# Three float32r products in place of one float32 product, in most projections of a four-layer attention kernel, under a new order of the work

## The reference

```
L0: x += proj(causal_attention(q,k,v of ln(x)));  x += proj(cross_attention(q of ln(x), k,v of context))
    x += gelu(ln(x) @ W_fc + b) @ W_mproj + b                       # 256 -> 1024 -> 256
L1: the same shape with layer norms behind the sums, relu, and a general mask in its self-attention
L2: cross-attention (q of x, k,v of context, a mask per element), 16 heads of 16, then layer norm
L3: cross-attention with 16 heads of 64: q = x @ w_q (256 -> 1024), k, v = context @ w_k, w_v (256 -> 1024),
    softmax(q k / 8) v, @ w_fc (1024 -> 256), plus x, then layer norm
```

## Time and profile before

| | us |
|---|---|
| median of 3 runs (4389.6 to 4390.9) | 4390.59 |
| span of the profiled execution | 4385.8 |
| PE busy | 4260.8 (97%) |
| DVE busy | 3663.2 (84%) |
| ACT busy | 2547.7 (58%) |
| POOL busy | 1590.0 (36%) |

### The profile page before, as it was taken

How to read it: one execution, slowest core, us unless ns; L and a number is a source line. 1 busy time by engine, 2 the same in 40 slices (tenths; PEclk the granted TensorE clock), 3 DMA queues, 4 the chain that set the end, 5 groups by cost and what they waited for, 6 DMA issues and landing times. The chain is left out here.

```text
span 4385.8 us, 99261 instructions
## 1 busy us (share of the span) xinstructions
PE 4260.8 (97%) x33536; PEld 3436.5 (78%) x33536; DVE 3663.2 (84%) x12709; ACT 2547.7 (58%) x6753; POOL 1590.0 (36%) x2709
## 2 busy tenths in 40 slices
PE   5999999999999899999999999999999999999998
PEld 3788888888887677777777777778888888888886
DVE  4899999999997899999999999967777777777774
ACT  2556656566565545455454554536676767676765
POOL 3445454454452234444444444431222222222222
PEclk8999999999999999999999999999999999999999
DMA  5555455554553544545444454433222222222220
GB/s 172 147 154 161 133 151 153 140 161 138 149 157 114 152 132 137 141 127 163 133 146 132 133 149 124 135 98 84 62 78 61 79 61 79 61 77 63 72 66 9
DMA packets 406443, 513.40 MB, mean 117 GB/s; under 512 B 133808, under 2 KB 373936, under 8 KB 384432
## 3 DMA queue, kind: packets, MB, share of 16 engines
q1 hardware_dynamic: 398544, 496.82, 39.7%
q10 hardware_dynamic: 7392, 10.24, 0.7%
HBM read 266.30 MB, written 236.72 MB: 115 GB/s over the span
## 5 line engine op out<-in xcount | busy, mean ns | idle before, releaser
L816 ACT ACTIVATE probs_own<-bank 128x384 f32<-128x384 f32 (+2 forms) x1280 | 644.6, 569 | 80.0 <-DVE bank L1065 41.7
L723 ACT ACTIVATE ht<-bank,columns_l 128x256 f32<-128x256 f32 x384 | 197.2, 569 | 729.4 <-PE bank L1242 726.3
L625 POOL TENSOR_SCALAR veps<-meanvar 128x2 f32<-128x2 f32 x256 | 63.9, 249 | 1357.1 <-DVE meanvar L966 1357.1
L1189 PE MATMUL bank<-ht,w_ff 128*128 128x256 f32 x2048 | 489.8, 382 | 2.7 <-ACT ht L723 1.6
L1189 PE MATMUL bank<-w_ff,ffh 128*128 128x256 f32 x2048 | 475.7, 380 | 0.0
L1046 DVE DVE_READ_ACCUMULATOR2_ANT nmf_own<- 128x1 f32 x3072 | 433.5, 141 | 0.0
L1189 PEld LDWEIGHTS bank<-w_ff,ffh 128*128 128x128 f32 x2048 | 378.7, 190 | 49.4 <-issue 1.2
L1046 DVE CUSTOM_DVE_ANT_0 bank<-bank,mask_rows 128x256 f32<-128x256 f32 x1024 | 398.8, 457 | 21.2 <-PE bank L1189 21.1
L1189 PEld LDWEIGHTS bank<-ht,w_ff 128*128 128x128 f32 x2048 | 369.6, 190 | 50.0 <-ACT ht L723 2.8
L1189 PE MATMUL bank<-kstack_own,qstack_own 96*128 96x256 bf16 (+2 forms) x3072 | 370.1, 248 | 27.2 <-DMA kstack_own<-k_parts 18.7
L881 ACT ACTIVATE probs_other<-bank,negmax 128x120 f32<-128x120 f32 x1024 | 356.6, 383 | 59.6 <-DVE negmax L1169 59.6
(11 more groups left out here) (164 smaller groups left out, 10138.4 us busy)
## 6 DMA issues: line engine op xcount, KB each, us to landing
qstack_own<-q_parts SPq DMA_DIRECT2D x96, 768.0 KB, 5.7
kstack_own<-k_parts SPq DMA_DIRECT2D x64, 768.0 KB, 7.3
qstack_other<-q_parts SPq DMA_DIRECT2D x64, 768.0 KB, 5.9
q_parts<-q_parts_own SPq DMA_DIRECT2D x96, 384.0 KB, 2.5
q_parts<-q_parts_own SPq DMA_DIRECT2D x96, 256.0 KB, 2.3
k_parts<-k_parts_own SPq DMA_DIRECT2D x64, 384.0 KB, 2.9
q_parts<-other_parts SPq DMA_DIRECT2D x64, 384.0 KB, 2.5
other_words<-k_parts SPq DMA_DIRECT2D x64, 360.0 KB, 3.3
```

The source lines that it names most:

```text
L625: nc.gpsimd.tensor_scalar(veps[key][:, :], meanvar[key][:, :, 1], r["norms"][key]["eps"], None, ALU.add).then_inc(veps_ready.sem, 1)
L723: return nc.scalar.activation(out, in_, ACT.Identity, scale=scale, bias=bias)
L816: nc.scalar.activation(probs[key][0:rows, j % a.slots, 0:n], bank_of(u)[0:rows, 0:n], ACT.Exp, scale=a.scale).then_inc(a_done.sem, 1)
L1189: return nc.tensor.matmul(out, lhsT, rhs, start=first, stop=True, skip_group_check=True)
```

## The change

Each float32 product `lhsT.T @ rhs` of the listed steps becomes three float32r products into the same PSUM bank: both operands are written as a high part of type float32r and a remainder, lo = x - hi, also float32r, and hi*hi + hi*lo + lo*hi is summed.

```diff
+        def mm3(out, lhsT, rhs, first):
+            mm(out, lhsT[0], rhs[0], first)
+            mm(out, lhsT[0], rhs[1], False)
+            return mm(out, lhsT[1], rhs[0], False)
```

```diff
-                        ins = mm(bank[:, m * T:(m + 1) * T], r["ff"]["w"][:, c, (2 * j + m) * P:(2 * j + m + 1) * P], x[:, c, :], c == 0)
+                        ins = mm3(bank[:, m * T:(m + 1) * T], (hi[:, c, at], lo[:, c, at]), (ht_hi["2"][:, c, :], ht_lo["2"][:, c, :]), c == 0)
```

The parts are made by new steps. Per element: ACT writes `ht_hi` from PSUM ahead of `ht`, and POOL subtracts:

```diff
+                    if key in r["split_ht"]:                      # "0" and "2" in l0 and l1, "1" in l2
+                        affine(ht_hi[key][:, 0, :], bank[:, 0:T], gain[:, 0:1], shift[:, 0:1])
+                        affine(ht_hi[key][:, 1, :], bank[:, T:2 * T], gain[:, 1:2], shift[:, 1:2])
                     affine(ht[key][:, 0, :], bank[:, 0:T], gain[:, 0:1], shift[:, 0:1])
...
+            elif kind == "ht_lo":                                 # POOL
+                for f in range(FT):
+                    ins = nc.gpsimd.tensor_tensor(ht_lo[key][:, f, :], ht[key][:, f, :], ht_hi[key][:, f, :].bitcast(F32), ALU.subtract)
...
+            elif kind == "rest3":                                 # DVE, 4 per element of l2
+                v.tensor_tensor(ot3_lo[:, 2 * j:2 * j + 2, :], bank, ot3_hi[:, 2 * j:2 * j + 2, :].bitcast(F32), ALU.subtract)
```

```diff
+            elif kind == "weights_hi":
+                act_e.wait_ge(arrived[key], ...)
+                for h, x in zip(hi, raw):
+                    ins = copy(h[:, :, :], x[:, :, :])
...
+            elif kind == "weights_lo":
+                        ins = nc.gpsimd.tensor_tensor(lo[n][:, c, :], raw[n][:, c, :], hi[n][:, c, :].bitcast(F32), ALU.subtract)
```

All of `LISTS` is new, for every engine and pass, and `SPREAD` is now (0, 1) throughout, so that the first and last elements of a pass are no longer corrected. A few places, old and new (time in element periods):

```diff
-START = {"l0": 0.0, "l1": 33.12879, "l2": 66.18842}
+START = {"l0": 0.00000, "l1": 32.95726, "l2": 66.42901}
 l0 PE
-            norm.0.0/0.24343 project_k.own.0/0.29714 ... negate_t.own.0/1.16618 ... norm.2.0/3.92324 ff_in.ff.0/3.97118 ... ff_out.ff.3/4.88122
+            norm.0.0/0.60700 project_k.own.0/0.82717 ... negate_t.own.0/1.71999 ... norm.2.0/4.37194 ff_in.ff.1/4.51158 ... ff_out.ff.3/5.45066
 l0 DVE
-            ff_in.ff.3/4.73013 ff_mid.ff.2/4.74993 ff_mid.ff.3/4.80456
+            ff_in.ff.2/5.17545 ff_mid.ff.2/5.27393 ff_in.ff.3/5.32873 ff_mid.ff.3/5.35967
 l1 PE
-            turn.0.0/0.09548 project_q.own.0/0.13496 ... negate_t.own.0/1.17403 ... norm.2.0/3.87252 ff_in.ff.1/3.92875 ... ff_out.ff.3/4.79026
+            turn.0.0/0.14969 project_k.own.0/0.28915 ... negate_t.own.0/1.70805 ... norm.2.0/4.20845 ff_in.ff.3/4.32439 ... ff_out.ff.3/4.92385
 l2 PE
-            ... probs_v3.three.3/3.66090 project_out3.three.2/3.72515 project_out3.three.3/3.76506
+            ... probs_v3.three.2/3.80393 project_out3.three.0/3.96077 ... project_out3.three.3/4.17756
 l2 DVE
-            project_out3.three.0/3.81120 stats.3.0/3.82783 norm.3.0/3.88660
+            rest3.three.1/3.56262 rest3.three.0/3.60038 rest3.three.3/3.89264 rest3.three.2/3.90734 project_out3.three.0/4.21786 stats.3.0/4.51278 norm.3.0/4.86170
```

More of the change, by code:

```diff
@@ L60 @@
         "PE": """
[L61 to L75, removed]
@@ L76 @@
-            probs_v.other.2/3.40602 probs_v.other.3/3.41650 project_out.other.0/3.64697 norm.2.0/3.92324 ff_in.ff.0/3.97118
-            ff_in.ff.1/4.08214 ff_in.ff.2/4.50058 ff_in.ff.3/4.56880 ff_out.ff.0/4.68899 ff_out.ff.1/4.77584 ff_out.ff.2/4.82853
-            ff_out.ff.3/4.88122
+            norm.0.0/0.60700 project_k.own.0/0.82717 project_q.own.0/0.86112 scores_max.own.4/1.28161 scores_max.own.11/1.29911
+            scores_max.own.9/1.30514 scores_max.own.7/1.31117 scores_max.own.2/1.38316 scores_max.own.5/1.43286
@@ L86 @@
[L86 to L90, removed]
@@ L92 @@
+            ff_mid.ff.2/5.19113 ff_in.ff.3/5.20549 ff_mid.ff.3/5.34441
         """,
         "DVE": """
[L94 to L106, removed]
@@ L144 @@
-            scores_exp.other.1/3.08000 scores_exp.other.5/3.08802 probs_v.other.0/3.32424 probs_v.other.1/3.33391
-            probs_v.other.2/3.34357 probs_v.other.3/3.35324 project_out.other.0/3.61110 norm.2.0/3.87252 ff_in.ff.1/3.92875
-            ff_in.ff.2/4.28344 ff_in.ff.0/4.39942 ff_in.ff.3/4.49575 ff_out.ff.0/4.65459 ff_out.ff.1/4.69327 ff_out.ff.2/4.75159
-            ff_out.ff.3/4.79026
+            turn.0.0/0.14969 project_k.own.0/0.28915 project_q.own.0/0.36215 project_v.own.0/1.17639 scores_max.own.0/1.23948
@@ L148 @@
+            probs_v.other.1/3.72375 project_out.other.0/4.00600 norm.2.0/4.20845 ff_in.ff.3/4.32439 ff_in.ff.0/4.40560
+            ff_in.ff.2/4.52839 ff_in.ff.1/4.58809 ff_out.ff.0/4.73628 ff_out.ff.2/4.80963 ff_out.ff.1/4.87757 ff_out.ff.3/4.92385
         """,
         "ACT": """
-            turn.0.0/0.11124 split_hi_q.own.0/0.17966 split_mid_q.own.0/0.23820 split_hi_k.own.0/0.27302
-            split_mid_k.own.0/0.38316 split_hi_k.other.0/1.13125 scores_exp.own.2/1.29684 scores_exp.own.1/1.30749
@@ L177 @@
-            negate.other.1/2.74174 negate.other.2/2.81011 negate.other.3/2.84852 negate_t.other.0/2.90492
-            project_v.other.0/3.21119 probs_v.other.0/3.36405 probs_v.other.1/3.37834 heads_rec.other.0/3.40659
-            heads_back.other.0/3.55262 project_out.other.0/3.67569 stats.2.0/3.70189 norm.2.0/3.79538 ff_out.ff.0/4.83497
-            stats.3.0/4.85109 norm.3.0/4.90957
+            split_rest_k.own.0/0.42105 split_rest_q.own.0/0.43791 project_v.own.0/1.24420 scores_max.own.0/1.26094
@@ L749, in _ @@
                     act_e.wait_ge(a_full.sem, w.value(a_full, u.tag))
+                if first and kind == "norm":
+                    reuse(act_e, w, u, xhat_ready, [("norm", "2", 0)], u.element - 1)
                 for count, tag in ahead["ht_users"][key](a_full, d_full):
@@ L885, in _ @@
                 if first and j == r["first_of"]["turn3"]:
-                    reuse(act_e, w, u, d_full, [("project_out", "other", 0)], u.element - 1)
+                    reuse(act_e, w, u, d_full, [("ff_out", "ff", i) for i in range(4)], u.element - 1)
                 if w.new(a_full, u.tag):
@@ L1427, in _ @@
                     for c in range(2 * j, 2 * j + 2):
-                        ins = mm(bank[:, t * C:(t + 1) * C], x[:, c, t * P:(t + 1) * P], wt[:, c, :], c == 0 and t == 0)
+                        ins = mm(bank[:, t * C:(t + 1) * C], ffh[:, c, t * P:(t + 1) * P], wt[:, c, :], c == 0 and t == 0)
+                ins.then_inc(d_full.sem, 1)
+            elif kind == "project_out3":
+                split("fc")
+                _, (hi,), (lo,) = r["split_weights"]["fc"]
+                if w.new(rest_ready, ("rest3", "three", j)):
+                    pe.wait_ge(rest_ready.sem, w.value(rest_ready, ("rest3", "three", j)))
+                bank = take(u) if j == 0 else bank_of(u, (kind, key, 0))
+                for t in range(QT):
+                    at = slice(t * P, (t + 1) * P)
+                    for c in range(2 * j, 2 * j + 2):
+                        ins = mm3(bank[:, t * C:(t + 1) * C], (ot3_hi[:, c, at], ot3_lo[:, c, at]), (hi[:, c, :], lo[:, c, :]), c == 0 and t == 0)
                 ins.then_inc(d_full.sem, 1)
@@ L1482, in sb, with shared @@
         return t[n]
+    def shared(*tensors):
+        for group in tensors[:-1]:
+            with ExitStack() as one:
+                for n, shape, dt in (group if isinstance(group, list) else [group]):
+                    t[n] = one.enter_context(nc.sbuf_tensor(n, shape, dt))
+        return sb(*tensors[-1])
     def each(keys, n, shape, dt=F32):
```

525 lines of the change are left out of this document (346 added, 179 removed), and 6 rows, old and new, of the table SPREAD.

## The result

The changed kernel takes 4535.7 us (median of 4 runs, 4533.4 to 4543.2) against 4390.1 before: ratio 1.0335, interval 1.0321 to 1.035. It is slower by 146 us, where 4205 was forecast.

A forecast was written before the change was run, and what follows sets the result against it. PE was taken to bound all three passes. Its 326 us saving, less 120 given back to DVE, left about 205: 4385.8 - 205 + 20 for edges = 4201, plus 4.8 for runs: 4205 us; own range 4150 to 4265, overall 4090 to 4330.

The forecast's parts named there:

- What bounds the kernel: All three passes: PE sets the pace, with periods of 41.9, 45.5 and 44.3 us per element.
- What PE saves: Products on PE: 330 us-thousandths (ns) instead of 430 or 445, saving 2.8 us per element in l0, l1 and 4.6 in l2.
- The keys' row: Context keys' float32 records on PE: pitch of 111 ns, taken as nearest evidence for 110 ns per pass at 256 columns.
- The saving of 327 us: All passes on PE: by the skill's rule three of four float32 passes remain, three quarters of the cost, saving about 327 us.
- What the others get: Added ACT, POOL and DVE steps: all hidden, none a bound; about 2.5 us more wait behind each transposition is covered.
- DVE is late next: DVE limits l0 and l1 once PE is faster, giving back 120 of PE's 326 us of saving.
- the floors of 40.6 and 44.5: Least us per element for DVE in l0 and l1: busy times 38.5 and 42.7 plus remaining idle time.
- The tanh wait: In l0, DVE's ffh waits 2.0 us per element for ACT's tanh; the new order was taken to leave half.
- The edges: Filling, changes of pass and draining: +8 us at the start and 12 for longer element ways, +20 us taken.
- Rival 4: All passes: the order eats the saving, PE's waits grow by 5 us per element, 4390 us and up; chance 0.05.
- Rival 2: DVE gets slower, POOL's added work stretching ffh in l0 and l1, and engines wait mutually: 4282 to 4359 us; chance 0.20.
- Rival 3: PE's float32r pass costs near 215 ns, not 110, deciding at 143: about 5050 us; chance 0.09.

The follow-up runs named there:

- y_neworder_old: Kernel before (plain float32 products, no splits) under the changed kernel's order, two project_v3 steps of l2 moved earlier: 4725.3 us, ratio 1.0764.
- m1_max_later: Changed kernel with the own maxima's first step on PE and DVE planned later in l0 and l1: 4549.4 us, ratio 1.0363.
- v_l2_only: Kernel before in its old order, with three float32r products and their splits in the third pass alone: 4379.3 us, ratio 0.9971.
- x_oldorder_new: Changed kernel's products and splits in the order of before, new steps put in and some nearby steps moved slightly: 4676.7 us, ratio 1.0656.
- v_l2_ff2: Kernel before, old order, float32r products in l2 and in l0's and l1's ff_in; l1's POOL stats.1.0 ahead of the xb steps: 4411.3 us, 1.0045.
- q1: Changed kernel with two POOL steps moved, l0's xb.0 behind the low part of ht and l1's low part of q earlier: 4535.5 us, ratio 1.034.
- v_l2_own: Kernel before, old order, with float32r products in l2 and for q, k, v of l0's and l1's first attention: 4583.5 us, ratio 1.0438.

## Why the prediction was wrong

**What bounds the kernel:** right for the kernel before. PE at 99.6% and more in each pass was the bound; that holds no hint of how little slack the loop behind it has.

**What PE saves:** the sign right, the size half. The 110 ns a pass came out as 0.12, but the first pass of each block of four products takes 0.20, so a product is 1.52/4 = 0.38 us, not 0.33. Seven blocks save 7 x 0.2 = 1.4 us per element in `l0` and `l1`, not 2.8. In `l2` blocks of four fell from 1.76 to 1.47 (queries) and from 1.73 to 1.52 us (output), the 512-wide ones of two from 1.77 to 1.47 (medians over 3400 to 3700 us): 4 x 0.29 + 4 x 0.21 + 2 x 0.30 = 2.6 us, not 4.6. The keys' row that I took a pass from was one long run and could not show the cost of a start. By the rule in the Trainium skill (FP8 and Floating Point Precision, "TensorE Precision Notes") three of four passes leave 0.75 of the time; measured is 1.52/1.72 = 0.88. The saving of 327 us that the prediction gives by that rule is also added up wrongly: its own terms make 64 x 28 x 0.1075 + 32 x (32 x 0.111 + 4 x 0.22), some 335.

**What the others get, the failed step:** "so the wait is covered", with the new lists' 0.22 and 0.14 periods, and for the new order nothing. Where that was looked up it was about right (no wait for `ht_lo` stands in PE's list in `l0` or `l1`), but it looked only at the added steps. The order around them had moved, and `y_neworder_old` shows the price of that without any of the new products: 2.5 and 3.8 us per element.

The loop of the own scores shows what became longer. This table splits its period at two points of PE, the last product for the own exponentials and the first for the next element's own maxima (starts, medians over the windows named under The experiments; in brackets the distances that PE's lists plan, in periods):

| us | l0 before | l0 changed | l0 `y_neworder_old` | l1 before | l1 changed | l1 `y_neworder_old` |
|---|---|---|---|---|---|---|
| last exponentials to both stacks landed | 12.1 | 9.9 | 9.2 | 9.4 | 10.9 | 10.0 |
| last exponentials to first maxima | 14.0 (0.34) | 9.9 (0.22) | 9.3 (0.22) | 10.8 (0.24) | 11.0 (0.19) | 10.0 (0.19) |
| first maxima to last exponentials | 27.9 (0.66) | 33.8 (0.78) | 34.8 (0.78) | 34.7 (0.76) | 37.4 (0.81) | 38.9 (0.81) |

Under the new order the maxima start the moment the stack has landed, so the first distance has nothing left to give, and the second is longer by 5.9 and 2.7 us. In `l1` the plan leaves 0.19 periods, 9.3 us, for a stack that has landed only after 10.9. The two stacking DMAs also changed places: before, the queries' was issued first (it landed in 6.1 us in `l0` and 5.5 in `l1`, the keys' behind it in 6.9 and 7.7); now the keys' is first (5.4 and 5.5) and the queries' second (7.6 and 8.9).

That this loop sets the period is argued, not shown. `m1_max_later` gave the first distance back (0.27 periods in both passes) and won 1.0 us in `l1`, but lost 1.3 in `l0`. What is shown is that the order as a whole costs 2.5 and 3.8 us, and that the prediction put it at nothing without comparing the distances of the two lists.

In `l2`, 40.2 us were forecast and 44.2 measured. The saving was 2.6 instead of 4.6, and PE idles 2.1 us per element, most for DVE's negated parts and the DMA of the negated rows. The old order with the same products has 43.4 (`v_l2_only`), so the order is 0.8 of it.

**DVE is late next:** the floors of 40.6 and 44.5 counted DVE's busy time of before. It became 40.4, 44.1 and 37.0 us per element, from 38.5, 42.7 and 33.0, and was reckoned unchanged but for 2.6 in `l2`. In the old order with the same products and splits (`x_oldorder_new`) it is 39.0, 43.7 and 35.1, in the new order without them (`y_neworder_old`) 40.1 and 43.8. So in `l0` most of the growth comes with the new order; in `l1` either alone brings about 1.1. DVE was busy for 92 and 91% in `l0` and `l1`, not the 94% and more that were to show the forecast right, and most of PE's idle time was for DMAs. The tanh wait did nearly halve: `ffh` for `ff_xu` 47.0 to 26.6.

**The edges:** +20 forecast, about -15 measured; no run was made for `SPREAD`.

**The rivals.** Rival 4, with a chance of 0.05, was the one: the order eats it all. PE's waits grew by 2.6, 4.1 and 2.1 us, not 5, for DMAs and DVE's negated parts rather than for banks. Its "the steps' succession is nearly the old one" was the wrong sentence. Rival 2's mechanism is there, in other steps than `ffh` (which got shorter, mean 737 ns for 932): POOL adding or subtracting two SBUF tensors stretches DVE's small steps, 0.9 us of the loop in `l0`. The Trainium skill (GPSIMD Engine Reference, "1. Specifications") names DVE instructions with two SBUF inputs, or in a mode that uses two ports. The 128x32 subtraction fits the first; the cast with one input, 644 for 181 ns, doesn't, and no run shows in which mode it is. Rival 3 is out: a pass stays under 143 ns.

**What stays open:** which of the new order's distances, in `l0` above all, is the shortest; no single move gave back more than 1.0 of the 2.1 and 3.1 us. Why `ff_in` still costs half a microsecond behind `v_l2_ff2` wasn't tried. Undoing `m1`'s `l0` part and `q1`'s `l1` part would by their periods give 4535 - 32 x (0.7 + 1.0), some 4480, an estimate that takes the moves as independent, and still slower than before.

## What to carry over

Where the bound engine gets faster, find the chains that return to a single buffer and compare their planned distances in both versions before the work of each engine is summed: a distance filled by a DMA can't be planned below its landing. Look at what stands behind new steps in their own engine's queue, above all if the bound engine waits for that: in `v_l2_own` 1 us more on ACT came with 4.5 us lost per element. Read several moves by pass, not by total, since a gain in one stage and a loss in another cancel, and repeat an unchanged order first to know what difference counts.

## What the runs showed that I had not expected

- A float32r pass of 256 columns takes 0.12 us in a row and 0.20 as the first behind other work, although each of its weight loads takes 188 ns. Right behind another float32r block (3534.33 us) the first takes 0.12 too.
- Behind 2.4 us of standing in 4, the granted clock fell to 0.50 for some 4 us once per element, in a kernel that never left 1.00 in steady state before.
- POOL's 128x256 addition beside DVE lengthens 128x32 steps there from 181 to 644 ns and from 192 to 673. POOL's own `ht_lo` is slow behind the same spot in `l0`: of its two steps one takes 0.73 us and the other 1.4. No run shows why.
- With the same instructions, PE's busy time per element rose from 41.8 to 43.3 us in `l0` of `y_neworder_old`. A float32 record of 256 columns lasts 0.38 us and the next starts 0.22 us behind its start, so a wait under 0.16 us leaves no idle time in the profile. Starts behind another kind of work cost some too (93 ns ahead of the first `probs_other` product of a block, in both kernels); how much of the 1.5 us is which was not separated.
